# Moving the two halves of a final product from steps 14 and 15 of a batch to steps 0 and 2 of the next, in a two-stage transformer kernel

## The reference

```
x = x + 0.5 * _L1_ffn_ref(_layernorm(x), w1, b1, w2, b2)
x = x + _L1_attn_ref(_layernorm(x), ...)      # 16 heads of width 8, softmax
x = x + 0.5 * _L1_ffn_ref(_layernorm(x), w1, b1, w2, b2)

def _L1_ffn_ref(x, w1, b1, w2, b2):
    h = relu(x @ w1 + b1)                     # 128 -> 512
    return h @ w2 + b2                        # 512 -> 128
```

## Time and profile before

| | us |
|---|---|
| median of 3 runs | 2091.82 (2090.67 to 2093.68) |
| the profiled execution | 2089.9 |
| its span | 2087.8 |
| TensorE, matmul busy | 1933.9 (93%) |
| TensorE, weight loads busy | 1335.6 (64%) |
| VectorE busy | 1537.2 (74%) |
| ScalarE busy | 1174.1 (56%) |
| GpSimd busy | 670.3 (32%) |

### The profile page before, as it was taken

How to read it: one execution, slowest core, us unless ns; L and a number is a source line. 1 busy time by engine, 2 the same in 40 slices (tenths; PEclk the granted TensorE clock), 3 DMA queues, 4 the chain that set the end, 5 groups by cost and what they waited for, 6 DMA issues and landing times. The chain is left out here.

```text
span 2087.8 us, 34428 instructions
## 1 busy us (share of the span) xinstructions
PE 1933.9 (93%) x12468; PEld 1335.6 (64%) x12468; DVE 1537.2 (74%) x3852; ACT 1174.1 (56%) x2215; POOL 670.3 (32%) x767
## 2 busy tenths in 40 slices
PE   3999999999999999999999478999999999999997
PEld 2888888888888888888888323444444444444443
DVE  5767686666767677676776168888888888888881
ACT  3444444444444444444443137888887888878874
POOL 2333343234333343333431212333333333333311
PEclk9999999999999999999999659999999999999998
DMA  3000000000000000000000122222222222222210
GB/s 125 6 11 11 1 11 11 11 1 11 11 11 11 1 11 11 11 11 1 11 6 6 36 78 90 84 85 85 86 82 79 85 85 85 79 81 85 80 47 11
DMA packets 49992, 85.81 MB, mean 41 GB/s; under 512 B 6752, under 2 KB 11104, under 8 KB 49760
## 3 DMA queue, kind: packets, MB, share of 16 engines
q1 hardware_dynamic: 47920, 81.85, 12.5%
q10 hardware_dynamic: 1904, 1.78, 0.3%
HBM read 49.26 MB, written 34.87 MB: 40 GB/s over the span
## 5 line engine op out<-in xcount | busy, mean ns | idle before, releaser
L1344 DVE TENSOR_REDUCE b_nm<-b_MX 128x1 f32<-128x512 f32 x1024 | 649.6, 683 | 101.8 <-PE b_MX L1459 93.7
L1235 ACT ACTIVATE b_pr<-b_ST 128x512 f32<-128x512 f32 x1024 | 550.1, 601 | 153.6 <-PE b_ST L1446 151.1
L410 ACT ACTIVATE s<-G 128x512 f32<-128x512 f32 x306 | 182.7, 597 | 350.9 <-PE G L714 348.2
L1459 PE MATMUL b_MX<-b_kt,b_qt 32*128 32x512 f32 x1024 | 350.4, 505 | 22.1 <-DMA b_qt<-staging 11.6
L719 PE MATMUL Y<-w_wd,h 128*128 128x128 f32 x2448 | 329.0, 277 | 17.4 <-DVE h L575 16.1
L1446 PEld LDWEIGHTS b_ST<-b_qt,b_kt 32*128 32x128 f32 x1024 | 126.7, 183 | 320.4 <-ACT b_pr L1235 209.8
L1446 PE MATMUL b_ST<-b_qt,b_kt 32*128 32x512 f32 x1024 | 313.1, 497 | 19.8 <-ACT b_pr L1235 18.7
L566 DVE TENSOR_TENSOR su<-U,s 128x512 f32<-128x512 f32 x272 | 187.0, 687 | 190.6 <-PE U L714 113.5
L719 PEld LDWEIGHTS Y<-w_wd,h 128*128 128x128 f32 x2448 | 305.8, 192 | 33.2 <-DVE h L575 23.9
L1474 PE MATMUL b_PV<-b_pr,b_va 128*32 128x512 f32 x2048 | 276.2, 612 | 0.0
L575 DVE TENSOR_TENSOR h<-C,su 128x512 f32<-128x512 f32 x272 | 188.0, 691 | 9.3
(11 more groups left out here) (246 smaller groups left out, 3492.4 us busy)
## 6 DMA issues: line engine op xcount, KB each, us to landing
b_kt<-staging SPq DMA_DIRECT2D x64, 256.0 KB, 2.8
b_qt<-staging SPq DMA_DIRECT2D x64, 256.0 KB, 3.4
staging<-b_khi SPq DMA_DIRECT2D x32, 256.0 KB, 3.0
staging<-b_qhi SPq DMA_DIRECT2D x32, 256.0 KB, 3.2
xin<-in_x SPq DMA_DIRECT2D x17, 256.0 KB, 2.9
mid<-xo SPq DMA_DIRECT2D x17, 256.0 KB, 2.0
b_x<-mid SPq DMA_DIRECT2D x16, 256.0 KB, 3.1
staging<-b_klo SPq DMA_DIRECT2D x16, 256.0 KB, 3.1
```

Source lines behind the costliest of these rows:

```text
L410: nc.scalar.activation(sbuf_s[n % 2][:], G[n % 2][:], ACT.Silu).then_inc(act_done.sem, 1)
L1235: nc.scalar.activation(pr[k % 2][:, j], bank[:].rearrange("p a b -> p (a b)"), ACT.Exp, scale=SM_SCALE).then_inc(used["st"].sem, 1)
L1344: nc.vector.tensor_reduce(nm[g % 2][:, c:c + 1], bank[:].rearrange("p a b -> p (a b)"), AX.X, ALU.max).then_inc(used["mx"].sem, 1)
L1459: pe.matmul(flat(MX[place % MX_BANKS]), qt[g][rows_of(j), u // HG % T], flat(kt_[g])[rows_of(j)], start=True, stop=True).then_inc(made["mx ...
```

## The change

Three edits. In `SMALL` the two halves of y leave the ends of steps 14 and 15, where they belong to the batch before, and go to the ends of steps 0 and 2, where they belong to the batch two before. `program` runs one batch further, so that the y of the last batch is done. In SP's queue the store of the result, with its wait, goes from the end of a batch to a place behind shift 1 of the next.

```diff
 SMALL = [
-    [], [("nm", 0, 1), ("ot", -1, 3)], [], [("xt", 1, 0)],
+    [("y", -2, 0)], [("nm", 0, 1), ("ot", -1, 3)], [("y", -2, 1)], [("xt", 1, 0)],
     [("kp", 1, 0)], [("nm", 0, 2), ("qp", 1, 0)], [("ot", 0, 0)], [("v", 1, 0)],
     [("ft", -1, 0)], [("nm", 0, 3), ("ot", 0, 1)], [("g", -1, 0)], [("g", -1, 1)],
-    [("g", -1, 2)], [("nm", 1, 0), ("g", -1, 3)], [("ot", 0, 2), ("y", -1, 0)], [("y", -1, 1)]]
+    [("g", -1, 2)], [("nm", 1, 0), ("g", -1, 3)], [("ot", 0, 2)], []]
...
-            for n in range(-2, batches + 1):
+            for n in range(-2, batches + 2):
                 batch_steps(Batch(n // 2, n % 2))
...
                 shift(B, 1)
+                done = B + -2
+                if done.exists:
+                    p = done.parity
+                    sp.wait_ge(used["y"].sem, done.at(used["y"], 2))
+                    sp.dma_start(od[done.number], res[p][:]).then_inc(stored[p].sem, 16)
                 stage_batch(nxt)
...
                 shift(nxt, 0)
-                if prv.exists:
-                    p = prv.parity
-                    sp.wait_ge(used["y"].sem, prv.at(used["y"], 2))
-                    sp.dma_start(od[prv.number], res[p][:]).then_inc(stored[p].sem, 16)
```

## The result

The changed kernel takes 2104.77 us (median of 4, 2103.88 to 2108.79) against 2092.75 for the kernel before (2090.67 to 2093.93): ratio 1.0066, interval 1.0049 to 1.0083. It is 12 us slower; 2093.5 with a range of 2088 to 2100 was forecast. A second comparison, made later beside other kernels, gave 2106.83 against 2094.41, ratio 1.0056 (1.0036 to 1.0075).

A forecast was written before the change was run, and what follows sets the result against it. Step by step, TensorE's order of work bounds steps with y and latency the bare ones. Terms 2.5 - 0.1 - 2.1 + 2.3 - 2.3 + 1.4 gave +1.7 us, so 2093.5, range 2088 to 2100.

The forecast's parts named there:

- What bounds a step: TensorE's order of work bounds steps with y (half y 1.98 us); a bare step is a latency loop of 2.66.
- Step 14 without y: Step 14, once y half 0 has left it, becomes 2.74 us.
- Batch 0's 3.34: Length of step 14 in batch 0, which has no y; taken as the other bound, 2.00 us saved over both steps.
- Step 15 without y: End of batch: PV waits at the ring's wrap for VectorE to drain the fourth MX product; step 15 takes 3.82 us.
- Steps 0 and 2 with y: Start of batch: each becomes 3.84 us, costing 1.08 and 1.18, since only 0.8 to 0.9 of 1.98 finds cover.
- SP, GpSimd, the shift of group 0: Moved store, loads and waits cost nothing; the shift gets less room, 0 with an upper bound of some 0.3 a batch.
- The sum over the batches: Steady batch +0.19; all batches 2.5 - 0.1 - 2.1 + 2.3 - 2.3 us, before the epilogue.
- The epilogue: After the last PV: y half 0 of batch 14 adds 1.1 us, the addition of half 1 adds 0.3; +1.4.
- the clock is granted in full in all of the steps: Read from the profile of the kernel before, for steps 14, 15 and 0 to 3; no cost was forecast for it.
- The rivals: Four cases: forecast 2093.5 us (chance 0.64), slower 2102 (0.20 with a smaller relative), faster 2086 (0.12), much faster 2060 (0.04).
- B: Ring neighbours hold TensorE in both steps, step 14 stays 3.34: 2102 us; chance 0.20 together with a missed fetch.
- D: VectorE is the bound and y on TensorE fits into bare steps 0 and 2 without cost: 2060 us; chance 0.04.

The follow-up runs named there:

- banks counted on: MX banks counted on from batch to batch at the ring's wrap: on the changed kernel 2078.27 us, ratio 0.9925; on the kernel before 2085.73, ratio 0.9956.
- five spare products: Changed kernel plus five spare 128x512 products on TensorE ahead of the first score of step 0, overwritten by that score: 2091.67 us, ratio 0.9997.
- second split: Against the kernel before, y half 0 stays at the end of step 14 and half 1 goes to step 0: 2091.60 us, ratio 0.9996.
- quarters at 14, 15, 0 and 2: Against the kernel before, y in four quarters at the ends of steps 14, 15, 0 and 2: 2069.99 us, ratio 0.9877.

## Why the prediction was wrong, point by point

- What bounds a step: right. TensorE's sums of 3.84 for a step with y and the latency loop of a bare step held within 0.01 in the steady batches of every kernel of the study, as long as the clock was full.
- Step 14 without y, 2.74: right (2.73 to 2.74, and batch 0 falls to it as well). Batch 0's 3.34 was rightly not taken.
- Step 15 without y: the mechanism was right (the ring's wrap, a wait for a maximum, none for b_res), the size 3.82 was 3.76. The banks counted on took this away (2.67).
- Steps 0 and 2 with y, +1.08 and +1.18, and step 3, +0.04: right in the batches with the full clock.
- SP, GpSimd, the shift of group 0: no cost seen; the shift is waited for once, 0.2 us, from 1300 to 2000.
- The sum over the batches, +0.3 without the epilogue: without the seven long steps it is 10.98 - 10.95 = 0.0. The kernel with five spare products, which is the change without the falls, measures 0.9997 of the kernel before; the forecast 1.0008 lies in its interval.
- The epilogue, +1.4: from the last PV to the end of the span 27.6 us with the spare products against 25.95 before, +1.7; in the two traces of the change +2.9, with half clock at the last PV, and +1.0. The size was about right, and one execution can't tell it better.
- The step that failed is the sentence that the clock is granted in full in all of the steps, from which every duration was carried over. The prediction found the wait of step 15 (1.4 us, and no other work of TensorE there) and priced it only as time lost in that step. It didn't ask what TensorE's clock does behind it. The missing term is 7 of 14 batches by 1.55 to 1.6 us, 10.95 us in one trace and 11.2 in the other, against 11.3 us between the forecast and the measured median. Batch 0, used as the check for step 15, has the same wait of 1.61 us and a step of 2.76 at full clock behind it; a single example couldn't show something that happens half of the time. No batch of the kernel before has a fall between the first steps and the last PV, so the price of one could not be read there, only that the condition was new.
- The rivals: none of the four was it. The 2104.8 lies past B's 2102, but by another cause: B's step 14 of 3.34 didn't come, and the fetch of group 0 was waited for in 4 batches again. D's steps 0 and 2 without a cost didn't come either (3.85 each).
- The Trainium skill, "TensorE: Matmul & The Clock Gate", Part 1, says that the throttled clock is the default state and that activity releases it. The traces agree: behind a step 15 in which TensorE is busy 3.73 of 3.75 us (five spare products) the clock stays 1.00, and behind one with 2.66 of 3.77 it falls to half in half of the batches. A rival built on that page should have stood in the prediction.

What stays open: why one batch is hit and the next, with the same rows, isn't; why the split with y in steps 14 and 0 is spared; and the fall in batch 0 with the banks counted on. The two runs of the changed kernel show that the batches vary from run to run, no more.

## What to carry to other kernels

When an edit takes work away from the end of a stage, look not only at what the stage then costs but at how busy TensorE is in it, and ask what follows at half clock: a wait of 1.4 us cost 1.55 more behind itself, in half of the cases. The slices of the page are too coarse for it; the granted clock has to be read step by step. Spare matmuls in a wait that was there anyway were free here (step 15 took 3.75 with and without them) and are a quick test of this cause. And a ring of buffers whose length isn't a multiple of the number of banks has one short distance at its wrap, worth 0.58 us a batch in the old order and 1.09 in the new one: count the banks on, or fill the ring up.

## What the runs showed of the hardware

- The granted clock fell to half behind 3.75 us in which TensorE was busy 2.66, with one wait of 1.44 us in it, in 7 of 14 places in each of two runs, and in 5 of 14 with 3.28 busy. It didn't behind 3.37 us with 2.72 busy (second split) nor behind 2.67 with 2.25 busy (banks counted on).
- How long it stayed low went with what followed: with y behind it, it was back within the step (mean 0.68 over 5.38 us); with bare steps behind it, it lasted into or through step 1, at the longest through a whole step of 4.79 us at 0.50 and into the next. A hit cost 1.5 to 1.6 us in the one case and 1.9 to 3.4 in the other.
- A wait for a transfer stood ahead of a fall too: in the kernels with five spare products, with the banks counted on and with quarters at 14, 15, 0 and 2, a step 8 of batch 6 stretched by the fetch of group 0 (3.92, 4.12 and 3.94 us instead of 2.76) was followed by a step 9 of 4.49, 4.49 and 4.38 instead of 3.33. It isn't fixed either: in the change a step 8 of 4.25 was followed by one of 3.34.
